# Constant products on TensorE ahead of the first keys and between the last projection and the experts

## The reference, cut to what matters

```python
def reference(x, ids, ctx, g_norm, Wq, Wkv, Wout, g_out, w1, w2):
    x = x + attention(layernorm(x), ...)   # 4 x 512 tokens, 512 wide; 16 heads of 128, one shared key and value head
    x = x + experts(layernorm(x), ids, ctx, ctx, ctx)  # 4 experts of 512, chosen by token id: silu(x Wg) * (x Wu) Wd
    x = x + ffn(layernorm(x), w1, w2)      # 2048 hidden, activations rounded to 8 bits, weights to -1, 0, 1
    return x
```

## Time and profile before

| what | value |
|---|---|
| median of 3 runs | 1084.36 us (1082.53 to 1085.66) |
| the profiled execution | 1088.8 us |
| its span, first to last instruction | 1087.1 us |
| mean granted TensorE clock | 0.956 |
| PE, DVE, ACT, POOL busy | 935.1, 743.1, 546.5, 206.0 us |
| instructions | 18880 |

### The profile page before, as it was taken

The page is one execution under the profiler, slowest core; times in us unless marked ns, Lnnn a source line. Parts: engine busy times, 40 slices in busy tenths (PEclk is TensorE's granted clock), DMA queues, the critical chain, the costliest instruction groups (busy, mean ns, idle before and its releaser), DMA issues.

```text
span 1087.1 us, 18880 instructions
## 1 busy us (share of the span) xinstructions
PE 935.1 (86%) x6538; PEld 519.7 (48%) x6538; DVE 743.1 (68%) x1637; ACT 546.5 (50%) x1517; POOL 206.0 (19%) x337
## 2 busy tenths in 40 slices
PE   0687889889999998999999999998942899569996
PEld 0344546545656564565665655664411344224442
DVE  4248896666877575778576767784421399889894
ACT  2557766766675674676667676753110221123330
POOL 1212211102221223132222121211320021101111
PEclk9989999999999998999999999999966899969999
DMA  9315645355576353555434444479349852216564
GB/s 265 84 39 117 146 108 120 96 145 127 150 171 165 108 120 86 135 124 116 113 91 117 105 108 106 105 156 189 107 120 214 165 112 49 49 24 146 131 126 97
DMA packets 305662, 131.85 MB, mean 121 GB/s; under 512 B 275232, under 2 KB 279840, under 8 KB 305568
## 3 DMA queue, kind: packets, MB, share of 16 engines
q1 hardware_dynamic: 301728, 118.03, 48.7%
q0 software_dynamic: 3840, 12.60, 3.4%
HBM read 42.76 MB, written 20.99 MB: 59 GB/s over the span
## 4 chain that ended last, share of the span: by engine, by line
PE 60%; DVE 17%; SPq 7%; ACT 6%; issue 5%; DMA 3%; POOL 2%; DVEq 1%; ACTq 0%; POOLq 0%
PE S L236 5%; PE S L238 5%; PE S L237 5%; PE QB L236 5%; PE QB L237 4%; PE QB L238 4%; PE S L644 4%; PE OUTB L236 4%; PE OUTB L237 4%; PE OUTB L238 4%; PE O L544 4%; PE O L542 4%; PE O L546 4%; SPq L430 3%; DVE P L1024 2%
## 5 line engine op out<-in xcount | busy, mean ns | idle before, releaser
L544 PE MATMUL O<-V,P 128*128 128x128 f16 x1024 | 179.2, 221 | 0.0
L542 PE MATMUL O<-V,P 128*128 128x129 f16 x1024 | 179.0, 219 | 0.0
L546 PE MATMUL O<-V,P 128*128 128x129 f16 x1024 | 178.9, 218 | 0.0
L1024 DVE TENSOR_TENSOR P<-P 128x1024 f16<-128x1024 f32 x128 | 156.8, 1225 | 4.4
L1012 DVE SCALAR_TENSOR_TENSOR QTOKR<-QB,rn,QTOKR 128x128 f16<-128x128 f32 x240 | 67.6, 344 | 119.6 <-ACT QTOKR L737 119.4
L756 ACT ACTIVATE OTOK<-O,rd 128x128 f16<-128x128 f32 x256 | 79.4, 365 | 132.9 <-DVE rd L1029 132.9
L745 ACT ACTIVATE P<-S,cst 128x1024 f32<-128x1024 f32 x128 | 140.0, 1130 | 12.0 <-PE S L238 11.5
L236 PE MATMUL QB<-WQA,XQA 128*128 128x512 f16 x240 | 93.5, 390 | 41.6 <-DVE QTOKR L1012 27.9
L1360 POOL TENSOR_SCALAR qst<-qs 128x4 f32<-128x4 f32 x64 | 18.2, 284 | 498.3 <-ACT junk L728 490.6
L544 PEld LDWEIGHTS O<-V,P 128*128 128x128 bf16 x1024 | 99.2, 97 | 7.4
L542 PEld LDWEIGHTS O<-V,P 128*128 128x128 bf16 x1024 | 98.4, 96 | 7.8 <-issue 0.3
(11 more groups left out here) (195 smaller groups left out, 1799.2 us busy)
## 6 DMA issues: line engine op xcount, KB each, us to landing
SIDE<-in_L_ffn_w_dram SPq DMA_DIRECT2D x64, 256.0 KB, 3.2
OTA<-sorted_rows SPq DMA_DIRECT2D x4, 1028.0 KB, 7.0
OTA<-in_L_attn_Wq_dram SPq DMA_DIRECT2D x4, 1024.0 KB, 11.6
SIDE<-in_L_attn_Wout_dram SPq DMA_DIRECT2D x16, 256.0 KB, 3.0
SIDE<-in_ctx_dram SPq DMA_DIRECT2D x16, 256.0 KB, 3.2
ctx_split<-SIDE SPq DMA_DIRECT2D x16, 256.0 KB, 2.7
ROWB<-in_x_dram SPq DMA_DIRECT2D x16, 256.0 KB, 3.3
w_tern<-SIDE SPq DMA_DIRECT2D x32, 128.0 KB, 2.9
```

The source lines that it names most:

```text
L542: nc.tensor.matmul(o, ph(g)[:, a:a + P], V[:, b % 2, j, 0:129], start=j == 0, stop=False)
L544: nc.tensor.matmul(o[:, 0:128], ph(g)[:, a:a + P], V[:, b % 2, j, 130:258], start=False, stop=False)
L546: last = nc.tensor.matmul(o, pl(g)[:, a:a + P], V[:, b % 2, j, 0:129], start=False, stop=j == NT - 1)
L1024: nc.vector.tensor_tensor(pl(g)[:, cols], P32[:, cols], ph(g)[:, cols], ALU.subtract).then_inc(p_lo, 1)
```

## The change

On TensorE 300 products of 128 columns, `onesb` against `lower`, into the bank `OUTB`, are put between the wait for `consts` and the first keys. Another 64, of 512 columns each, `onesb` against stretches of the output weights `WOA`, into the bank `QB`, are put behind the last `outputs`, ahead of the waits of the experts; they wait for `q_lo`, which is the last query block's. No semaphore is incremented by them. Nothing else changes, on any engine.

```diff
+            def warm_small(n):
+
+                for _ in range(n):
+                    nc.tensor.matmul(OUTB[:, 0:P], lower[:, :], onesb[:, :], start=True, stop=True)
+
+            def warm_wide(n):
+                pe.wait_ge(q_lo, STEPS)
+                for i in range(n):
+                    a = (i % 16) * 512
+                    nc.tensor.matmul(QB[:, :], onesb[:, :], WOA[:, a:a + 512], start=True, stop=True)
+
             pe.wait_ge(consts, 1)
+            warm_small(300)
             keys_values(0)
             keys_values(1)
...
             for n in range(STEPS - HEADS, STEPS):
                 outputs(n)
+
+            warm_wide(64)
```

## The result

The changed kernel takes 1089.87 us in the median (8 runs, 1087.86 to 1093.9) against 1085.1 for the kernel before (8 runs, 1082.53 to 1087.69); the ratio is 1.0054 with a 95% interval of 1.0034 to 1.0075. It is slower by some 5 us, where no change was forecast. Timed again with the experiments the same kernel gave 1.0019 (0.9996 to 1.0042), 1087.29 against 1083.97 us in the medians. Both intervals hold 1.0034 to 1.0042, about 4 us, but the second one also holds 1; the size is known no better than that.

The account below looks back on a forecast made before the run. The chain ending last was taken as the bound, 60% TensorE, but DMA and SyncE's queue before the keys and first down. Terms 0 + 0 + 0 = 0 left the median at 1084.4 us, range 1081.0 to 1086.8.

Parts of the forecast that it names:

- The small products: Start, before the keys: 300 products end at 22.8, the clock falls again, keys start at 1.2 GHz; term 0.
- Where a clock falls behind a stop: TensorE's clock falls 2.4 to 5.0 us behind a stop, the longest shorter than the rest of 5.2 to 5.9 us before the keys.
- The first rival: Start: small products end nearer the input, rest at most 5.0 us, keys start warm, 2.0 us won, median 1082.3; chance 0.15.
- The wide products: Turn to the experts: 64 take 14.1 us at most, ups warm and up to 2.9 us sooner, first down unmoved; term 0.
- The stated sign of being wrong: Turn to the experts: prediction wrong if last output product to first down isn't 53.7 us; one of three such signs.
- The step that failed is the one on code: Code fetches: at most some 3 packets more, 0.2 us if all fell between 11 and 28 us, 0 elsewhere; taken as 0.
- The rivals: Keys start warm (0.15), small products run past the input (0.04), ups in the path after all (0.03).
- the one that ended on the slower side: Start: clock doesn't rise under small products, or not for long; at 107 ns keys 7.1 us late, 1091.5; chance 0.04.
- the chance of 0.07 for slower: Whole kernel: chance given to a measurement slower by more than about 0.3%, 3.3 us; within had 0.88, faster 0.05.

Follow-up runs that it names:

- the small half: The changed kernel without the 64 wide products, only the 300 small ones at the start: 1085.66 us against 1083.4 before, ratio 1.002.
- the wide half: The changed kernel without the 300 small products, only the 64 wide ones: 1085.8 us, ratio 1.0034; timed again 1087.08 against 1083.97 us, ratio 1.0006.
- the kernel with 108 products: Against the kernel before: nothing added at the start, 108 small products of 128 columns at the turn to the experts, no wide ones: 1089.17 us, ratio 1.0039.
- 20 harmless products: 128 instead of 108 small products at the turn, nothing else added to the kernel before: 1083.2 us, ratio 0.9991, against 1089.17 us with 108.
- 24 that stopped 3.3 us short: Kernel before plus 34 wide products before the keys, 70 small at the turn, 24 of 512 columns before the first down: 1081.27 against 1084.15 us, ratio 0.9973.

## Why the prediction was wrong

**The small products** (300, ending at 22.8; keys cold): right. They ended at 22.19, and the clock was down again before the keys. In two other kernels with the 300 the clock rose later, and they ended at 23.0; the keys were cold there too.

**Where a clock falls behind a stop**: the conclusion was right, the bound was not quite. Here it took 5.4 us, where 5.0 was the longest seen, and 2.85 in the small half; nothing hung on it, as the rest was 7.14 us. The first rival counted on at most 5.0 us as a bound, which was no bound.

**The wide products**: right in the steps, with 14 us, a warm clock for the ups, and a first down that a DMA releases. The stated sign of being wrong, a distance of other than 53.7 us from the last output product to the first down, did come about, with 56.4, but it says nothing of these products: from the last output product to the first down the profiles with wide products have 53.3 to 56.4 us (six), those without 53.1 to 56.1 (six, before's 53.7 among them).

**The step that failed is the one on code**: "at most some 3 packets more, 4 us of one DMA engine out of 16. On the path it would be 0.2 us if it all fell between 11 and 28 us, and 0 elsewhere. I take 0." Two things were wrong in it.

The volume was divided by 16 engines. A fetch is one packet of 16 KB (0.9 to 2.2 us of one engine in these traces), and a transpose with one in it lands 1.3 to 1.7 us later, as the tails show. At the start the issue at line 370 has 8.47 to 8.50 us in the nine profiles in which no code is fetched by 28 us, and 9.01 to 9.43 in the five with two fetches there. The first key comes at 28.92 in the mean of these five, and at 28.24 in that of the nine others: 0.7 us, three times and more what was allowed. This was the small term. It is shown less well than the tail: the first keys of the two groups nearly touch (28.65 before, 28.68 in two of the five), and the five are also the ones with small products running there, so no run tells the fetches from those products at the start. Why one packet holds up a transfer spread over 16 engines is argued, not seen: such a transfer may be done only when its last part is, and the engine with the packet would be the late one.

And "0 elsewhere" took the count of fetches for all that could change. Every fetch behind an insertion moves, the 54 old ones too. The rows before had a tail whose last fetch happened to lie well, and in which TensorE rested 0.6 and 1.8 us. This is the term that was missing: 1.7 us of a later transpose, and 2.6 us of a clock that falls in the longer rest, together 4.3.

The sum by steps is then 0.7 + 4.3 = 5.0 us, against 4.8 in the medians and 3.3 when measured again. That it comes so near to the first is in part luck: the steps are read from one execution, the middle part between them scatters by 7.6 us, and in the five profiles with small products at the start it is on the short side (738.5 to 740.5 us), which no run explains.

The rivals were all built on the two stretches that the change touches, and the one that ended on the slower side (small products past the input) rested on another mechanism, which didn't come about: the clock rose 3.4 us behind their start. So the chance of 0.07 for slower stood on that and on the scatter.

What stays open is the wide half alone, at +0.3% once and +0.1% once; the 1.5 to 3 us by which the kernel with 108 products is slower than its tail explains; and the scatter of the middle part.

## What to carry to other kernels

An insertion into a long unrolled program is also a move of all the code behind it. Where an effect of a few microseconds is unexplained, look at where the code queue's packets fall in the trace, above all beside the last transfers that an engine waits for; pad to a whole piece (here 256 instructions) and time again before anything else is concluded. Someone who times an idea of 0.3% in such a program measures the padding as well: here 20 harmless products made 5 to 6 us of difference.

A few wide products keep the clock up with less code than many small ones. The 34 of 512 columns that brought the keys to full clock are 68 instructions and no fetch ahead of the keys, while 384 small ones were 768 and three. They have to run close up to the moment at which the real work can start: the 34 that stopped 0.4 us short served, and so did the 64 that stopped 2.8 us short of the ups; the 300 that stopped 7 us short did nothing, as did 24 that stopped 3.3 us short.

## What the runs showed of the hardware

A small transfer of code is not small for a big one beside it: 16 KB fetched during a transpose of 512 KB put it off by 1.4 to 1.7 us (5.43 and 5.42 us from VectorE's end to TensorE's start in the changed kernel, 5.09 with 108 products, 3.72 before, where no fetch was in it).

The clock turned 1.7 us of longer rest into a loss of 4.3. The length of the rest alone doesn't tell whether it falls: a rest of 2.56 and 2.57 us before the last 16 products left it up (the two profiles of the wide half), one of 2.55 let it fall (the small half).

Products with one and the same weight load repeated ran like any other of 128 columns: 0.056 us apart at full clock, as the value products with 0.057, and 384 in 24.44 us with the first 57 at half clock.
